# Two attentions in one transformer layer: pairing row-tiled logits, and overlapping the last Q projections with the second attention

## The reference, cut to what matters

```
x = x + attn_a(ln(x))      # 8 heads of two 64-wide halves; cosine logits L1, L2
    #  G = tanh(gain * (L1 - L2));  A1 = softmax(L1 + G);  A2 = softmax(L2 - G)
    #  y = (A1 - lambda * A2) @ v,  RMS norm, output projection;  no mask
x = x + ffn(ln(x))         # one 1024x1024 product (weights rounded to int4) + a rank-16 product
x = x + attn_b(ln(x))      # 16 heads of 64, rope, causal mask, softmax, output projection
x = x + ffn(ln(x))
```

## Time and profile before

| | us |
|---|---|
| median of 3 runs | 1699.84 (1698.51 to 1876.04) |
| the profiled execution | 1698.39 |
| its span, core 7 (slowest) | 1695.3 |
| spans of the eight cores | 1689.4 to 1695.3 |
| mean granted TensorE clock, core 7 | 0.963 |

### The profile page before, as it was taken

The page is one execution under the profiler, slowest core; times in us unless marked ns, Lnnn a source line. Parts: engine busy times, 40 slices in busy tenths (PEclk is TensorE's granted clock), DMA queues, the critical chain, the costliest instruction groups (busy, mean ns, idle before and its releaser), DMA issues.

```text
span 1694.8 us, 40429 instructions; the slowest of 8 cores (1689.4 to 1695.3 us)
## 1 busy us (share of the span) xinstructions
PE 1527.1 (90%) x13344; PEld 787.2 (46%) x13344; DVE 1045.2 (62%) x1936; ACT 1271.2 (75%) x1908; POOL 533.7 (31%) x1089
## 2 busy tenths in 40 slices
PE   4999978899999999999999997859997899989978
PEld 2444434455555555555555554324443344434443
DVE  5464568878788887878878787533625444324215
ACT  4848569899999999999999997103335688778990
POOL 4000025444445454444545445522623000001001
PEclk9999989999999999999999999879997799989999
DMA  9724032111111111110112131553006132211302
GB/s 207 124 50 125 2 78 103 36 38 32 51 19 45 38 35 47 33 56 13 45 43 51 57 45 44 94 115 67 1 1 110 32 82 73 73 60 39 104 8 78
DMA packets 130460, 99.57 MB, mean 59 GB/s; under 512 B 98755, under 2 KB 114371, under 8 KB 130262
## 3 DMA queue, kind: packets, MB, share of 16 engines
q1 hardware_dynamic: 112902, 82.13, 17.7%
q0 software_dynamic: 17360, 14.88, 6.3%
HBM read 67.81 MB, written 20.97 MB: 52 GB/s over the span
## 4 chain that ended last, share of the span: by engine, by line
PE 44%; ACT 23%; issue 12%; DVE 4%; DMA 2%; POOL 1%; ACTq 0%; DVEq 0%; POOLq 0%; SPq 0%
ACT E L175 12%; PE pL L164 9%; ACT Gt L175 7%; PE pY L171 7%; PE pBb L164 6%; PE pB L164 4%; PE pS L166 4%; ACT EB L175 4%; PE pYb L171 4%; PE pL L166 4%; PE pD L164 3%; PE pS L164 1%; DVE Sx L184 1%; DMA xn<-xn 1%; PE pL L171 1%
## 5 line engine op out<-in xcount | busy, mean ns | idle before, releaser
L184 DVE TENSOR_TENSOR Sx<-pL,Gt 128x512 f32<-128x512 f32 x768 | 503.2, 684 | 138.0 <-PE pL L951 53.8
L175 ACT ACTIVATE E<-Sx 128x1024 bf16<-128x1024 f32 (+1 forms) x512 | 433.2, 846 | 15.2 <-DVE Sx L184 14.4
L175 ACT ACTIVATE EB<-pS,cst 128x1024 bf16<-128x1024 f32 (+1 forms) x320 | 296.6, 990 | 68.1 <-PE pS L166 65.5
L175 ACT ACTIVATE Gt<-pD 128x512 bf16<-128x512 f32 x512 | 306.8, 599 | 24.0 <-PE pD L164 15.1
L171 PE MATMUL pY<-V,E 128*128 128x129 bf16 x4096 | 308.2, 221 | 11.0 <-ACT E L175 2.1
L171 PEld LDWEIGHTS pY<-V,E 128*128 128x128 bf16 x4096 | 259.7, 98 | 92.5 <-issue 40.1
L166 PE MATMUL pL<-Q,K 64*128 64x256 bf16 x1536 | 198.8, 274 | 23.8 <-ACT E L175 15.6
L164 PE MATMUL pD<-Qn,K 128*128 128x256 bf16 x1024 | 196.3, 273 | 19.9 <-ACT Gt L175 12.5
L189 POOL TENSOR_SCALAR st<-st 128x1 f32<-128x1 f32 x64 | 17.8, 279 | 493.9 <-DVE st L426 477.3
L175 ACT ACTIVATE E<-pL 128x512 bf16<-128x512 f32 x256 | 154.2, 602 | 5.9 <-PE pL L171 0.9
L166 PE MATMUL pS<-Q,K 64*128 64x512 bf16 (+3 forms) x640 | 122.6, 377 | 22.2 <-ACT EB L175 17.3
(11 more groups left out here) (166 smaller groups left out, 2173.9 us busy)
## 6 DMA issues: line engine op xcount, KB each, us to landing
x<-xN SPq DMA_DIRECT2D x32, 512.0 KB, 4.8
x<-x SPq DMA_DIRECT2D x32, 512.0 KB, 3.2
out<-x SPq DMA_DIRECT2D x16, 512.0 KB, 2.9
x<-fker SPq DMA_DIRECT2D x3, 2048.0 KB
x<-WoT SPq DMA_DIRECT2D x2, 2048.0 KB
xn<-xn SPq DMA_DIRECT2D x16, 256.0 KB, 2.1
w_k<-WkT POOLq DMA_DIRECT2D x2, 1024.0 KB, 43.1
w_v<-WvT POOLq DMA_DIRECT2D x2, 1024.0 KB, 55.1
```

What stands on the lines that cost most here:

```text
L175: q.add(lambda e: e.activation(out, in_, func, **kw))
L184: q.add(lambda e: e.tensor_tensor(out, a, b, op))
```

## The change

In the first attention, `step_L` is called only in odd iterations, for two steps at a time, behind the background's matmuls; `step_S` comes before `step_Y`; both copies of `y_out` are made in a unit's first iteration, and the held-back `step_Y` comes behind the background of its own iteration; the background's credit is 2.6 in even and 0.6 in odd iterations, not 1.6 in each.

In stage 3 the Q groups of tiles 2 and 3 are taken out, and so is the barrier. They become a generator `last_q`, whose first group is issued before the second attention and whose other 15 are the background of its first units, in one bank (pY0), with pY1 for the permutation. It ends with the issue of the `WoB` load. The buffers of rope live on through stage 4.

In stage 4 the units of tile 1 and tile 0 alternate; then comes tile 2, then tile 3 as two groups of 256 queries, in which a step holds two key blocks. The 16 first units use two banks of Y without alternation, later ones three. `after_b` of a group joins the background six steps after its last unit, and `ffn` waits four steps after the transposes of its input are issued.

```diff
-    pL = [ps(f"pL{i}", p2) for i in range(4)]
+    pS = [p2.enter_context(nc.psum_tensor(f"pL{i}", [128, 2, QT], F32)) for i in range(2)]
+    pL = [pS[i // 2][:, i % 2, :] for i in range(4)]
...
         step_tanh(s + 2)
         step_exp(s)
+        step_S(s + 1)
         u, k = (s - NKS) // NKS, s % NKS
-        if u < 0 or k == 0 or k >= 3:
-            step_Y(s - 1)
-        elif k == 2:
-            step_Y(s - 2)
+        late_Y = u >= 0 and k == 1
+        if not late_Y:
             step_Y(s - 1)
         step_D(s + 3)
-        step_L(s + 2)
         step_A(s + 1)
-        if u >= 0 and k == 1:
+        if u >= 0 and k == 0:
+            y_out(u, 0)
             y_out(u, 1)
-        step_S(s + 1)
         if s >= 0:
-            bg.step(1.6, 2.6)
+            bg.step(0.6 if s % 2 else 2.6, 3.2)
+        if late_Y:
+            step_Y(s - 1)
+        if s % 2:
+            step_L(s + 2)
+            step_L(s + 3)
         if u >= 0:
-            if k == 0:
-                y_out(u, 0)
...
-        for t in reversed(two):
-            for h in range(HA):
-                group_q(t, h)
-        while late:
-            late.pop(0)()
-    phase_barrier()
-    p2.close()
+        if pair == 0:
+            for t in reversed(two):
+                for h in range(HA):
+                    group_q(t, h)
+            while late:
+                late.pop(0)()
+            rope_tok = po.done()
+            x_free[0] = x_free[1] = ve.done()
+    w3_dead = pe.done()
+
+    def last_q(*tiles):
+        nonlocal w_bank
+        for t, h in itertools.product(tiles, range(HA)):
+            i = h % 2
+            pe.wait(w_bank, w_tok[h // 4], xs_tok[t])
+            for c in range(NCH):
+                mm(pe, pY[0][:, :], Wo[:, c, 128 * h:128 * (h + 1)], xs[t][:, c, :],
+                   c == 0, c == NCH - 1)
+                yield 1
+            p_tok = pe.done()
+            yield 0
+            ac.wait(p_tok, qb_free[i])
+            act(ac, qb[i][:, :], pY[0][:, :], AF.Copy)
+            b_tok = ac.done()
+            yield 0
+            pe.wait(b_tok, pss_free[1])
+            mm(pe, pY[1][:, :], perm[:, :], qb[i][:, :], True, True)
...
+            w_bank = ve.done()
...
+            yield 0
+        state["rope"] = po.done()
+        p_tok = pe.done()
...
+        po.wait(p_tok)
+        for hf in range(2):
+            state["WoB"] = sl_w[0].start(po, Wo[:, :, 512 * hf:512 * (hf + 1)],
+                                         w_cols(di["WoB"], 512 * hf, 512))
...
+    w_bank = pss_free[0]
+    pair1_q = last_q(3, 2)
+    for _ in range(NCH):
+        next(pair1_q)
...
+    groups = [(QT, QT), (0, QT), (2 * QT, QT), (3 * QT, QA), (3 * QT + QA, QA)]
...
+    units = [(*gr, c) for c in range(HB // 2) for gr in groups[:2]]
+    units += [(*gr, c) for gr in groups[2:] for c in range(HB // 2)]
...
     def y_bank(i, k):
-        return (2 * i + k) % 3
+        return k if i < HB else (bank_of[i] + k) % 3
...
-            bg.add(after_b(t, [yn_tok[v] for v in range(i - c, i + 1)]))
+            toks = [yn_tok[v] for v, un in enumerate(units) if un[:2] == (q0, nq)]
+            bg.later(6, lambda: bg.add(after_b(q0, nq, toks)))
+
+    bg.gens.append(pair1_q)
```

More of the change, by code:

```diff
@@ L1 @@
 import contextlib
+import itertools
 import math
@@ L839, in turn_ln @@
         sy.wait(a_tok, xT_free.get(slot))
+        xT_clock[b] = bg.clock + state["lag"]
         xT_tok[b] = xm_free[i] = r_turn.next(sy).turn(
@@ L846, in ffn @@
         xt = xnT[:, :, 128 * slot:128 * (slot + 1)]
-        while b not in xT_tok:
+        while b not in xT_tok or bg.clock < xT_clock[b]:
             yield 0
@@ L917, in build_program @@
     state["ln3"] = True
+    state["lag"] = 0
+    xT_clock = {}
     bg = Background()
@@ L1281, in build_program, with after_b @@
     rb = [sb(f"rb{i}", (128, 8), F32, s4) for i in range(2)]
[L1282 to L1286, removed]
+    y_banks = [pD, pB, pY[1]]
+    y_free = [x_free[0], x_free[0], None]
+    ac.wait(w3_dead)
     state["ln3"] = False
-    for hf in range(2):
-        wo_tok = sl_w[0].start(po, Wo[:, :, 512 * hf:512 * (hf + 1)],
-                               w_cols(di["WoB"], 512 * hf, 512))
+    state["lag"] = 4
     out_tok = [None] * NTB
-    x_free = [None] * 4
-    xm_free = [None] * 4
     xT_tok.clear()
     xT_free.clear()
-    for b in range(4):
+    groups = [(QT, QT), (0, QT), (2 * QT, QT), (3 * QT, QA), (3 * QT + QA, QA)]
+    t_order = [q0 // 128 + i for q0, nq in groups for i in range(nq // 128)]
+    for b in t_order[:2]:
         load_x(d_x2, b)
[L1300 to L1304, removed]
+    def after_b(q0, nq, y_toks):
+        bs = range(q0 // 128, (q0 + nq) // 128)
+        for b in bs:
+            yield from out_proj(b, y_toks, state["WoB"], False)
             layer_norm(b, ve, b % 4, lambda a_tok, b=b: turn_ln(b, b % 4, a_tok, b % 4))
-        for b in four:
+        for b in bs:
             yield from ffn(b, b % 4)
@@ L1309, in after_b, with key_blocks @@
             out_tok[b] = x_free[b % 4] = r_st.next(sy).start(sy, rows_of(d_out, b), x[:, b % 4, :])
[L1310 to L1318, removed]
+            for v in t_order[t_order.index(b) + 4:][:1]:
+                load_x(d_x2, v)
+    steps = []
+    bank_of = []
+    n_banks = 0
+    units = [(*gr, c) for c in range(HB // 2) for gr in groups[:2]]
+    units += [(*gr, c) for gr in groups[2:] for c in range(HB // 2)]
+    for i, (q0, nq, c) in enumerate(units):
+        n = QT // nq
+        last = (q0 + nq) // 128 // n - 1
+        for p in range(last + 1):
+            steps.append((q0, nq, c, i, [n * p + k for k in range(n)], p == last))
+        bank_of.append(n_banks)
+        n_banks += nq // QA
+    NB = len(steps)
     S_tok, E_tok, Y_tok, m_tok, yn_tok = {}, {}, {}, {}, {}
-    y_free = [None] * 3
-    def q_lo(t, j):
-        return max(0, 128 * j - QT * t)
+    def key_blocks(s):
+        q0, nq, _, _, js, _ = steps[s]
+        return [(jj, j, max(0, 128 * j - q0)) for jj, j in enumerate(js)]
     def stepb_S(s):
@@ L1327, in stepb_S @@
             return
[L1328 to L1334, removed]
+        q0, nq, c, _, _, _ = steps[s]
+        pe.wait(E_tok.get(s - 2), rope_tok if s == 0 else None)
+        if s < 2:
+            pe.wait(*pqk_free[2 * s:2 * s + 2])
+        if q0 == 2 * QT:
+            pe.wait(state["rope"])
+        for jj, j, lo in key_blocks(s):
+            for hd in range(2):
+                rows = slice(64 * hd, 64 * (hd + 1))
+                mm(pe, pS[s % 2][:, hd, nq * jj + lo:nq * (jj + 1)],
+                   K[rows, c, 128 * j:128 * (j + 1)], Q[rows, c, q0 + lo:q0 + nq], True, True,
+                   (64 * hd, 0))
         S_tok[s] = pe.done()
@@ L1339, in stepb_exp @@
             return
-        t, c, j = blocks[s]
-        q0 = q_lo(t, j)
+        q0, nq, c, _, _, _ = steps[s]
         e = EB[s % EB_RING]
         ac.wait(S_tok[s], Y_tok.get(s - EB_RING))
-        act(ac, e[:, :, q0:QT], pS[s % 2][:, :, q0:QT], AF.Exp, scale=0.125, bias=shiftb)
-        E_tok[s] = ac.done()
[L1346 to L1349, removed]
+        kb = key_blocks(s)
+        parts = [(0, QT)] if all(lo == 0 for _, _, lo in kb) else \
+            [(nq * jj + lo, nq * (jj + 1)) for jj, _, lo in kb]
+        for lo, hi in parts:
+            act(ac, e[:, :, lo:hi], pS[s % 2][:, :, lo:hi], AF.Exp, scale=0.125, bias=shiftb)
+        E_tok[s] = ac.done()
+        for jj, j, lo in kb:
+            if 128 * j >= q0:
+                at = nq * jj + lo
+                ve.wait(E_tok[s])
+                tt(ve, e[:, :, at:at + 128], e[:, :, at:at + 128], rows_bc(tri[:, :], 2), OP.mult)
+                m_tok[s] = ve.done()
     def y_bank(i, k):
-        return (2 * i + k) % 3
+        return k if i < HB else (bank_of[i] + k) % 3
     def stepb_Y(s):
@@ L1381, in norm_b @@
         ve.wait(ve.done())
-        for k in range(2):
-            y = pYb[y_bank(i, k)][:, 0:4 * VB]
+        for k in range(nq // QA):
+            y = y_banks[y_bank(i, k)][:, 0:4 * VB]
             tt(ve, split(flat(ytb[i % 3][:, 2 * k:2 * k + 2, :]), 4),
@@ L1404, in build_program @@
         if 0 <= s - 2 < NB:
[L1405 to L1409, removed]
+            if steps[s - 2][5]:
+                turn_b(s - 2, norm_b(s - 2))
         if s >= 0:
```

60 lines of the change are left out of this document (40 added, 20 removed).

## The result

| | before | changed |
|---|---|---|
| median of 20 runs, us | 1701.01 | 1679.5 |
| ratio, with its 95% interval | | 0.988 [0.985, 0.991] |
| forecast | | 1635 (1602 to 1669) |

The change is faster, by 20 us (1.2%) and not by 65; the forecast was wrong and its range too. In the profiled execution (1701.66) two cores of one half of the chip ran at a lowered clock, so the rows of the changed kernel are those of core 7, in the other half, with a span of 1673.5, and all comparisons of versions use executions without such a disturbance, in which the changed kernel's median is 1678.2.

The account below looks back on a forecast made before the run. PE was taken to bound steps with background, ACT those without. Savings of 33 us in the first attention and 30 from 105 + 6 + 256 + 43 = 410 against 440.3 gave 1632, 1635 with 3.1 outside; range 1602 to 1669.

Parts of the forecast that it names:

- I take 3.09: First attention: a pair of steps with background takes 3.09 us, saving 0.15 on each of 193 pairs, 29 us.
- The first rival: First attention gives nothing because DVE, busy 2.6 of 3.2 us a pair, becomes the gate: 1668 us; chance 0.14.
- The 0.5 us per group end: First attention: about 0.5 us saved at each of 8 group ends, the background being done one step earlier.
- The estimate from the Trainium skill: First attention: with 166 ns per tiling-mode crossing, 0.33 us saved a pair, leaving ACT alone as the bound.
- Phase A: Second attention's first 16 units, tiles 1 and 0, with Q of tiles 2 and 3: 105 us (bounds 96 and 118).
- my 13.8: Phase A: price in us of a pair of units with background, 12.8 plus 0.5 at each unit for bank waits.
- The wait for a free bank of Y: Phase A, only two banks of Y: some 1 us, mostly covered by background and S; 0.5 added at each unit.
- Diagonal ones about 0.8: Phase A's last 18 steps, without background: 12 diagonal steps at about 0.8 us, 6 full ones at 1.0.
- WoB's wait of 3 to 5 us: Before the first output projection PE waits 3 to 5 us for the WoB load, which lands after 20.5 us.
- The stretch behind it: From the end of phase A to the end of the last unit, tiles 2 and 3: 262 us.
- the 6 us put down for WoB and its clock: After phase A: PE's wait for WoB plus 2 us for a lowered clock, 6 us (bounds 0 and 12).
- About 3 us exposed, twice: Tail: two blocks, not four, cover the way from output projection to feed-forward; tail stays at today's 43 us.

Follow-up runs that it names:

- thin_stats: Changed kernel with the first attention's layer-norm statistics taken over 32 of each 512 columns, result incomplete; eight units 97.8 us against 100.4.
- s_pairs_copy: `tail_merged` with DVE's sums issued in pairs, the second sum in a unit's first iteration behind the two copies of Y; 1652.5 and 1653.7 us.
- first_only: Kernel before with only the first attention's loop of the change; 1683.0 us against 1698.0, ratio 0.991 [0.989, 0.993].
- l_single: Changed kernel with the logits of each step issued in its own iteration, not in pairs; 1695.4 us, ratio to the kernel before 0.998 [0.997, 0.999].
- q_ahead: `tail_merged` with all 16 Q groups of tiles 2 and 3 issued ahead of the second attention, without a barrier; 1670.6 us, 9 more than `tail_merged`.
- tail_merged: Changed kernel with tile 3's four blocks as one background group: four output projections, then four feed-forwards; 1661.2 us, ratio to the kernel before 0.978 [0.977, 0.980].

## Why the prediction was wrong

**First attention: right saving, wrong bound.** The saving was read rightly: two crossings of about 0.10 fewer per pair of steps. The step that failed is "I take 3.09", a saving of 0.15 for each pair with background: it lets nearly all of PE's 0.20 through, as if PE alone set the pace. (The sum doesn't close either: 2.86 plus 0.18 is 3.04, and the "little off" would go below that.) Measured are 2.1 us per eight units, or 0.075 for each of the 28 pairs with background, half of what was forecast: 3.17 a pair by the prediction's own accounting. What stands in its place is DVE's queue, as `thin_stats` and `s_pairs_copy` show. The first rival had this mechanism; I gave it 0.14 and put it at no gain at all, where it takes half. What spoke for it stood in the sum: L needs the two sums directly before it, and DVE's queue is in order, so a background operation that falls between them can be paid by PE. The 0.5 us per group end for an earlier end of the background didn't come either; PE waited there for the transposes `Q<-yt` instead (3.9 us in 7 waits from 330 to 1030, before 0.6 in one). Of 33 us 15 came, in the trace and in `first_only`.

**The estimate from the Trainium skill**, which took the fixed part of a single matmul, 166 ns (TensorE: Matmul & The Clock Gate, Single matmul latency), for the price of a crossing, isn't borne out: rows of the changed kernel still show about 0.1 on leaving. The Trainium skill says that a change of tiling mode drains TensorE (TensorEngine Tiling (Array Packing), Tiling Modes, Key Properties); the loss of 0.10 at each crossing in the earlier trace rows agrees with it. `l_single` doesn't price a crossing: its 17 us are 0.07 for each of the 256 pairs, what came through of 0.20.

**Phase A: 118.8 for 105.** Three terms were too small. The entry: the first pair of units took 1260.3 - 1240.9 = 19.4 us, 5.6 over my 13.8. I had forgotten the first Q group's 8 matmuls (1.8 us) and the start itself: PE waits 2.5 us for exp, in four waits, and then runs 3 us at a clock of 0.50. Pairs with Q: (1334.2 - 1260.3) / 5 = 14.8, one more each. The wait for a free bank of Y was priced right (`ytb`, 4.8 us over the five pairs, for 1.0 a pair); the term put at nothing is the two others, for exp (3.1) and for the single bank of Q (`ro`, 2.5). The last two pairs: 12.75 each, 25.5 against 22.5 for both. "Diagonal ones about 0.8" is the step that failed there; `q_ahead` shows 1.0 on average over all widths. The clock was at 0.50 from 1347 on (rows above), in a stretch of such steps without background, so the low clock of the earlier trace rows wasn't the barrier's doing alone; whether the steps are slow by the clock or by their chain of waits is open. WoB's wait of 3 to 5 us was not to be seen (0.74, and for `ytb`): the load went out at 1342 and landed after 14.9 us and not 20.5, and the first output projection came 19 us behind it.

**The stretch behind it:** 258.8 for 262, partly by luck. Tile 2 took 114.6 for 115.5. Tile 3's two groups took 66.3 and 77.8, together 144 for 140, and the 6 us put down for WoB and its clock didn't come.

**Tail: 55.1 for 43.** "About 3 us exposed, twice" failed. The exposed way is 6.2 and 6.5 us, 6.7 more than that: in the trace DVE scales block 12 (`xn`, at 1628.3) only behind the statistics of block 13, and its transposes, issued at 1629.3, land 3.1 us later; the second pair of blocks does the same. And I left out the clock: by the same matmuls' times at either level some 5 us in all (3.59 for 1.89 and 1.01 for 0.61 after each wait, and the next 8 still 2.47 after the first). `tail_merged` takes both away and gains 17.

So of the 44 us between 1635 and 1679.5, 18 are the first attention, 14 phase A and 12 the tail; 3 came back behind phase A, 1 went in stage 3, and the rest is that core 7 of the profiled execution isn't the slowest core of the median one.

## What to carry to other kernels

Where engines are close, removing work from the first can hand the path to another: before taking a share of the saving, list for the waiting instruction what stands ahead of its releaser in that engine's queue. Work of independent blocks that covers a latency (normalise, transpose, multiply) has to be counted in blocks; splitting the last group in two halved its cover here and exposed it twice, for 17 us. The two waits of 6.2 and 6.5 us on TensorE cost their length and then half speed for the next 8 matmuls; price both. An edit that changes several things gets a version without each of them: the overlap, which looked like the second half's point, was 10 us of 27.

## What the runs showed that I had not expected

Bunching the same background matmuls (2.6 and 0.6 credits instead of 1.6 and 1.6) is worth 2.4 us per eight units. Without background, a step of the second attention on the diagonal took as long as a full one: in `q_ahead`, at a clock of 0.57, a unit of four diagonal steps 3.9 to 4.2 us, one with four full steps before them 7.9. The clock stayed near its lower level while PE's records cover most of the time: busy 21.4 of 24 us at 0.57 in `q_ahead`.
